# Macaron block (FFN, quaternion memory, FFN): the memory's output bias moved from a TensorE product into the centred output weights

## The reference, cut to what matters

```python
B, L, D = x.shape                      # 2, 4096, 256
keys = (x @ Wk.T + bk).reshape(B, L, N_QUAT, 4)
keys = keys / jnp.maximum(knorm, NORM_EPS)
values = (x @ Wv.T + bv).reshape(B, L, N_QUAT, 4)
bound = quat_mul(values, keys)
memory = jnp.cumsum(bound, axis=1)
retrieved = quat_mul(memory, quat_conj(keys)).reshape(B, L, D)
retrieved = retrieved / jnp.sqrt(positions)[None, :, None]
mu = jnp.mean(retrieved, axis=-1, keepdims=True)
var = jnp.var(retrieved, axis=-1, keepdims=True)
normed = (retrieved - mu) / jnp.sqrt(var + LN_EPS) * ln_g + ln_b
return x + (normed @ Wo.T + bo)
```

## Time and profile before

| | us |
|---|---|
| three runs, median (lowest to highest) | 648.37 (646.26 to 649.11) |
| the profiled execution, its own time | 648.11 |
| its span, first to last instruction | 646.4 |

### The profile page before, as it was taken

How to read it: one execution, slowest core, us unless ns; L and a number is a source line. 1 busy time by engine, 2 the same in 40 slices (tenths; PEclk the granted TensorE clock), 3 DMA queues, 4 the chain that set the end, 5 groups by cost and what they waited for, 6 DMA issues and landing times.

```text
span 646.4 us, 12285 instructions
## 1 busy us (share of the span) xinstructions
PE 612.6 (95%) x3341; PEld 521.1 (81%) x3341; DVE 565.1 (87%) x1168; ACT 468.2 (72%) x858; POOL 539.8 (84%) x626
## 2 busy tenths in 40 slices
PE   6989999999987999999999999998877999999997
PEld 5878989989865787777878787777666899898996
DVE  6979999998869999999999999999848788787773
ACT  5666776767567888888888888887365777677662
POOL 4588898897848999999999999998826988889863
PEclk9989999999999999999999999999899999999999
DMA  8740000000000000000000000000000110110111
GB/s 251 238 132 1 0 0 0 0 0 1 1 1 1 1 2 0 0 0 0 0 0 0 0 0 0 0 1 0 2 0 2 67 65 32 65 65 32 65 66 66
DMA packets 19273, 18.66 MB, mean 29 GB/s; under 512 B 1328, under 2 KB 19248, under 8 KB 19248
## 3 DMA queue, kind: packets, MB, share of 16 engines
q1 hardware_dynamic: 19248, 18.36, 8.8%
HBM read 9.97 MB, written 8.39 MB: 28 GB/s over the span
## 4 chain that ended last, share of the span: by engine, by line
PE 45%; POOL 25%; issue 18%; DVE 7%; ACT 3%; POOLq 1%; DMA 0%; DVEq 0%; ACTq 0%
PE bank L1228 25%; PE bank L1259 16%; POOL rhalf L286 7%; POOL ret L293 6%; POOL kact L275 5%; POOL bhalf L268 4%; PE bank L1242 4%; POOL bhalf L266 1%; ACT xn L778 1%; POOL rhalf L284 1%; DVE xk L410 1%; POOL xr_lo L1084 1%; DVE xn L613 1%; DVE kact L418 0%; POOL rstd L1077 0%
## 5 line engine op out<-in xcount | busy, mean ns | idle before, releaser
L1259 PE MATMUL bank<-wffn,kact 128*128 128x256 f32 x512 | 118.0, 384 | 6.5 <-DVE kact L418 4.1
L1318 PE MATMUL bank<-wkv,m_xnT 128*128 128x256 f32 x480 | 116.4, 385 | 2.4 <-ACT m_xnT L882 2.4
L1259 PEld LDWEIGHTS bank<-wffn,kact 128*128 128x128 f32 x512 | 96.0, 192 | 19.5 <-DVE kact L418 4.5
L1318 PEld LDWEIGHTS bank<-wkv,m_xnT 128*128 128x128 f32 x480 | 88.8, 190 | 24.2 <-ACT m_xnT L882 8.8
L299 POOL TENSOR_TENSOR xk_lo<-xk,xk_hi 128x1024 fp32r<-128x1024 f32 x30 | 71.1, 2370 | 43.7 <-ACT xk_hi L786 43.4
L1091 POOL TENSOR_TENSOR res<-res,gating_buffers 128x1024 f32 (+1 forms) x31 | 74.6, 2408 | 13.5 <-DVE gating_buffers L425 13.0
L1084 POOL TENSOR_TENSOR xr_lo<-xr,xr_hi 128x1024 fp32r<-128x1024 f32 x32 | 76.0, 2374 | 7.6 <-ACT xr_hi L792 6.2
L613 DVE TENSOR_TENSOR xn<-bank,khat 128x1024 f32<-128x1024 f32 x64 | 77.7, 1216 | 2.2
L778 ACT ACTIVATE xn<-res,shift,rstd 128x256 f32 (+1 forms) x128 | 66.5, 592 | 15.3 <-POOL shift L1079 11.0
L613 DVE TENSOR_TENSOR gating_buffers<-bank,khat 128x1024 f32<-128x1024 f32 x64 | 77.4, 1211 | 0.0
L1228 PE MATMUL bank<-wffn_hi,xr_hi 128*128 128x256 f32 x256 | 72.1, 282 | 0.0
(11 more groups left out here) (135 smaller groups left out, 1603.8 us busy)
## 6 DMA issues: line engine op xcount, KB each, us to landing
res<-x SPq DMA_DIRECT2D x15, 512.0 KB, 4.2
out<-res SPq DMA_DIRECT2D x15, 512.0 KB, 2.9
res<-x SPq DMA_DIRECT2D x2, 256.0 KB, 2.9
out<-res SPq DMA_DIRECT2D x2, 256.0 KB, 2.2
wffn<-w_k SPq DMA_DIRECT2D x1, 256.0 KB, 4.6
wffn<-w_r SPq DMA_DIRECT2D x1, 256.0 KB, 5.3
wo<-w_o SPq DMA_DIRECT2D x1, 256.0 KB, 5.6
wffn<-w_v SPq DMA_DIRECT2D x1, 256.0 KB, 5.8
```

What stands on the lines that cost most here:

```text
L1259: last = nc.tensor.matmul(dst[:, i, :], x[:, f, i * P:(i + 1) * P], wffn[:, w, f, :], start=f == 0, stop=f == FC - 1)
L1318: last = nc.tensor.matmul(dst[:, i, :], m_xnT[:, f, i * P:(i + 1) * P], wkv[:, f, col:col + D], start=False, stop=f == FC - 1, skip_group_ ...
```

## The change

The bias is added without a product of its own. The row of the bias, divided by 256, is added to each of the 256 rows of `wo_centred`. To the transposed `normed` one is added in each element. The product is then normed @ W + 1 @ W + normed @ bias/256 + 1 @ bias/256 = normed @ W + 0 + 0 + bias, since each column of W sums to zero, and each row of `normed` must now sum to zero too. For that `normed` is shifted as well as scaled, by `n_shift` = -mean x `n_rstd`, which DVE computes behind the reciprocal.

- PE: L1376 falls away (two products a step). One product of 128 x 256 is added behind L1401, which writes the bias as a row into every partition of PSUM.
- DVE: `ln_inverse` gets a wait on its own reciprocal and one `scalar_tensor_tensor` of 128 x 2 (inputs `n_mv` and `n_rstd`, both in SBUF); `rstd_done` is now signalled by that one. `other_layernorms` gets a wait on PE's new product and two `scalar_tensor_tensor` of 128 x 256, from PSUM and SBUF into `wo_centred`.
- ACT: `ret_normalize` gets a bias operand of one column; `evict_nT` turns from a copy into an Identity activation with a bias of one.
- POOL: one memset at setup.

```diff
@@ ln_inverse (DVE) @@
                 def ln_inverse(j, b):
                     dve.wait_ge(m["std_done"], 2 * j + b + 1)
-                    nc.vector.reciprocal(n_rstd[:, b, :], n_std[:, b, :]).then_inc(m["rstd_done"], 1)
+                    nc.vector.reciprocal(n_rstd[:, b, :], n_std[:, b, :]).then_inc(m["inverse_done"], 1)
+                    dve.wait_ge(m["inverse_done"], 2 * j + b + 1)
+                    nc.vector.scalar_tensor_tensor(n_shift[:, b, :], n_mv[:, b, :, 0], -1.0, n_rstd[:, b, :],
+                                                   ALU.mult, ALU.mult).then_inc(m["rstd_done"], 1)
@@ other_layernorms (DVE) @@
                 x_scales(1, CT, NT - CT)
                 memory_stats(NJ - 1, 1)
+                dve.wait_ge(out_bias_summed, 1)
+                for f in range(FC):
+                    nc.vector.scalar_tensor_tensor(wo_centred[:, f, :], bank[3][:, 0, 0:D], 1.0 / D, wo_centred[:, f, :],
+                                                   ALU.mult, ALU.add).then_inc(mem_ready, 1)
@@ ret_normalize, evict_nT (ACT) @@
-                        last = nc.scalar.activation(normed[:, i, :], ret[:, b, i, :], ACT.Identity, scale=n_rstd[:, b, i:i + 1])
+                        last = nc.scalar.activation(normed[:, i, :], ret[:, b, i, :], ACT.Identity, bias=n_shift[:, b, i:i + 1],
+                                                    scale=n_rstd[:, b, i:i + 1])
-                    nc.scalar.copy(normedT[:, :, :], rt_bank).then_inc(m["normedT_done"], 1)
+
+                    nc.scalar.activation(normedT[:, :, :], rt_bank, ACT.Identity, bias=one[:, 0:1]).then_inc(m["normedT_done"], 1)
@@ prepare (POOL) @@
+                nc.gpsimd.memset(one[:, :], 1.0)
@@ output (PE) @@
+                    pe.wait_ge(mem_ready, 2 * FC)
                     need(pe, m["x_done"], s)
                     for i in range(2):
                         for f in range(FC):
-                            nc.tensor.matmul(o_bank[:, i, :], normedT[:, f, i * P:(i + 1) * P], wo_centred[:, f, :],
-                                             start=f == 0, stop=False)
-                        last = nc.tensor.matmul(o_bank[:, i, :], ones[:, :], bias3[:, 2 * D:], start=False, stop=True)
+                            last = nc.tensor.matmul(o_bank[:, i, :], normedT[:, f, i * P:(i + 1) * P], wo_centred[:, f, :],
+                                                    start=f == 0, stop=f == FC - 1)
                     last.then_inc(m["O_done"], 1)
@@ first_values (PE) @@
                     nc.tensor.matmul(bank[3][:, 1, :], ones[:, :], bias3[:, 0:2 * D], start=True, stop=True).then_inc(kv_bias_summed, 1)
+                    nc.tensor.matmul(bank[3][:, 0, 0:D], ones[:, :], bias3[:, 2 * D:], start=True, stop=True).then_inc(out_bias_summed, 1)
```

More of the change, by code:

```diff
@@ L164, in macaron @@
         n_rstd = sb("n_rstd", [P, 2, 2])
+        n_shift = sb("n_shift", [P, 2, 2])
+        one = sb("one", [P, 1])
         m_xn = sb("m_xn", [P, 2, D])
@@ L217, in macaron @@
         kv_bias_kept = sem("kv_bias_kept")
+        out_bias_summed = sem("out_bias_summed")
         lnb_folded = sem("lnb_folded")
@@ L233, in macaron @@
         ffn_sems = [{n: sem(f"f{i}_{n}") for n in FFN_SEMS} for i in range(2)]
-        MEM_SEMS = ["x_st_done", "x_mv_done", "x_moments_done", "x_var_done", "x_power_done", "x_std_done", "x_rstd_done", "x_scales_done", "st_done", "mv_done", "std_done", "rstd_done", "xn_done", "T_done", "xnT_done",
+        MEM_SEMS = ["x_st_done", "x_mv_done", "x_moments_done", "x_var_done", "x_power_done", "x_std_done", "x_rstd_done", "x_scales_done", "st_done", "mv_done", "std_done", "inverse_done", "rstd_done", "xn_done", "T_done", "xnT_done",
                     "res_done", "K_bias_done", "V_bias_done", "K_done", "V_done", "ksq_done", "ksum_done", "above_done", "knorm_done",
```

## The result

The kernel after takes 664.02 us, the median of four executions (662.82 to 664.55), where the kernel before took 648.74 beside it (646.26 to 649.18). The ratio is 1.0241, with a 95% interval of 1.0211 to 1.0271. The forecast was 664.4.

What follows compares the result with a forecast made beforehand. DVE was taken to bound the memory stage. From 648.1 us, 14.5 for the shift, 1.6 for the bias row, 0.3 for ACT and -0.2 for PE gave 664.3, stated as 664.4, range 656.5 to 667.5.

Steps and rivals of the forecast that it cites:

- What bounds the stage: Memory stage: DVE bounds it, so added DVE work is paid in full 32 times and PE's saving is worth nothing.
- ACT's longer forms: Bias operands in ret_normalize and evict_nT: 0.3 us a step, hidden by ACT's idle time; 0.3 us in the last step.
- The -0.2 for the product in the peeled steps: Bias product ahead of the last but one store_x, where DVE waits for PE: removing it saves 0.2 us.
- The hold: Shift instruction in ln_inverse, held to POOL's next start: 0.49 us in each of 26 steps, 12.8; chance 0.75.
- steps 1 and 2: First two memory steps, POOL in another phase: 0.33 us for both, bounds 0 and 1.0.
- steps 28, 30 and 32: Late memory steps with POOL about to run dry or idle: 0.2, 0.24 and 0.25 us for the shift.
- The Trainium skill's rule that I weighed: VectorE with two SBUF inputs contends with GpSimd reading SBUF; the second is blocked for the other's whole instruction.
- step 31: Last but one memory step: POOL's instruction begins ahead of the new one, so the shift costs 0.69 us, unheld 0.22.
- The bias row: Between first FFN and memory: PE's new product and two DVE instructions delay key_sum 1.6 us, bounds 0.8 and 2.0.
- The mark that I gave for it: Sign for the bias row at the memory's start: key_sum starts near 193.3, where it was 191.67.
- The rival without the hold: Shift instruction of 128x2 not held, costing its own 0.22 to 0.25 us a step: 657.2 us; chance 0.13.
- Four fp32 products are 0.86: PE's output, 0.97 us a tile: four fp32 products take 0.86, so the bias product takes 0.11.

Runs made afterwards that it cites:

- b_stat128: Kernel before plus one bn_stats over 128 columns of wkv on DVE ahead of the reciprocal; 657.54 us, ratio 1.0129.
- b_no_product: Kernel before without its 64 bias products of output, the output bias left out; 646.04 us, ratio 0.9989.
- a_no_shift: Kernel after without the shift's wait and instruction on DVE, a column of zeros as ACT's bias; 651.87 us, ratio 1.0068 against the kernel before.
- a_psum_input: Kernel after with the new instruction's first input read from PSUM instead of n_mv in the memory's steps; 661.04 us, ratio 1.0208 against the kernel before.
- a_stat128: Kernel after plus one bn_stats over 128 columns of wkv on DVE ahead of the reciprocal; 668.26 us, ratio 1.0306 against the kernel before.
- a_stat384: Kernel after plus one bn_stats over 384 columns of wkv on DVE ahead of the reciprocal; 686.2 us, ratio 1.0591 against the kernel before.
- a_warm: Kernel after with idle products in PE's two gaps, 12 behind the bias row, 5 and 9 near the end; 665.63 us, ratio 1.028 against the kernel before.
- a_shift_on_act: Kernel after with the shift computed on ACT, DVE keeping the reciprocal alone; 653.32 us, ratio 1.0077 against the kernel before.
- a_pad4: Kernel after plus four one-column memsets on DVE ahead of the reciprocal; 667.8 us, ratio 1.0325 against the kernel before.

## Why the prediction was right, point by point

**What bounds the stage: right, and shown.** DVE bounds the memory steps. 0.20 us put on it cost 0.20 a step (b_stat128), and PE's products taken away gained nothing there (b_no_product). ACT's longer forms cost nothing in the steps: recip 1 to 27 is unchanged in a_no_shift, where they are in. They measured 587 ns for `normed` and 691 for `normedT` (493 and 588 before), as the same form had foretold. At the end of the stage they were to cost 0.3 us, and behind the last reciprocal a_no_shift has 0.29 over before. The -0.2 for the product in the peeled steps is there as well: b_no_product's last step is 9.64 us for 9.86.

**The hold: right, and shown.** The steps were to be 9.03 us and are 9.02, the new instruction 0.4 to 0.5 us and is 0.42, POOL's wait 0.7 and is 0.73. From the first to the 27th reciprocal I had 12.1 us more and there are 12.09. That match is closer than its parts: steps 1 and 2 cost 0.64 us where I had 0.33, and the 24 behind them 11.45 (0.48 each) where I had 11.76. a_psum_input separates the instruction's own 0.22 from the hold's 0.26; a_stat128 and a_stat384 show that it goes by POOL's boundaries. Over all 32 steps the hold applied where POOL was at work, and in steps 28, 30 and 32, with POOL idle, the instruction took 0.16 us. The Trainium skill's rule that I weighed, "SBUF — State Buffer", section "Who interferes with whom", held: with two inputs in SBUF the small instruction was blocked (0.42 us), with one it was not (0.16). In step 31 the forecast was 0.69, and it is there on DVE:

```profile
481.35 0.72 POOL L296 TENSOR_TENSOR ret<-rhalf 128x256 f32<-128x256 f32 x1
...
481.47 0.62 DVE L588 SCALAR_TENSOR_TENSOR n_shift<-n_mv,n_rstd 128x2 f32<-128x2 f32 x1
482.01 0.73 DVE L413 SCALAR_TENSOR_TENSOR xk<-diff,cols_less_one,bank 128x512 f32<-128x512 f32 x1
```

**The bias row: right in size.** DVE's wait and the two instructions, and PE's product ahead of them (timeline):

```profile
189.74 0.27 PE L1415 MATMUL bank<-bias,ones 128*128 128x256 bf16 x1
...
190.05 0.75 DVE L739 SCALAR_TENSOR_TENSOR wo_centred<-bank,wo_centred 128x256 f32<-128x256 f32 x2 [0.82 <-PE bank L1415]
190.73 0.68 DVE L600 TENSOR_REDUCE ksum<-ksq 128x128 f32<-128x512 f32 x1
```

From the first x_mv to key_sum it is 0.29 us in the kernels with the old start and 1.85 to 1.88 in all those with the new one. That is 1.58 in the kernel after, where I had 1.6. The mark that I gave for it, key_sum near 193.3, was missed all the same: it starts at 190.73, since the stage ahead of it ended 2.5 us earlier.

**What lies ahead of the memory: missed.** I took the stage ahead as fixed. It was 2.5 us shorter (x_mv at 188.86 for 191.38), and not by the change: b_no_product, whose edits lie in the memory alone, has the same. The traces show two causes, and neither comes from the change. One is the held `eps_pos`. The other is the clock: behind PE's idle time at 34 to 38 us of the span it was 0.50 between 38 and 40 us in four of the fourteen profiled executions, and 1.00 in the other ten. The products at that place in a_psum_input and in a_warm (timelines of PE):

```profile
36.09 5.41 PE L1275 MATMUL bank<-wffn,kact 128*128 128x256 f32 x16 [1.89 <-DVE kact L421]
```

```profile
37.74 3.72 PE L1272 MATMUL bank<-wffn,kact 128*128 128x256 f32 x16 [2.03 <-DVE kact L421]
```

Between POOL's second and third update of `res` there are 11.10 to 11.12 us in the four executions with the lower clock and 9.86 to 9.87 in the ten without. From that third update to x_mv it is 135.8 to 136.0 us in all fourteen. The four combinations all occur. With both causes (before, b_stat128, a_shift_on_act) x_mv starts at 191.4 to 191.5; with the hold alone (a_warm) and with the clock alone (a_psum_input) at 190.0; with neither, in nine kernels, at 188.0 to 188.9. So each is worth 1 to 2 us, and kernels whose code up to there is nearly the same differ in which of them they have. What makes the one or the other happen in an execution isn't settled. The length of PE's idle time ahead of the products isn't what decides, since the clock fell behind 1.89 us and not behind 2.03.

**PE's clock at the two ends: missed.** The forecast had nothing for it. From key_sum to the first reciprocal it is 0.5 us in the kernel after, and in the table 0.5 to 1.5 in every kernel with the bias row against 0.0 to 0.2 in those without. In all of the former but a_warm PE is idle for 3.29 us ahead of its transposes, and the clock falls to 0.50 behind it; how long it stays there differs. a_warm kept the clock, but its 0.7 us come from idle products that ended late, so no run gives the price of the idle time at the start by itself. For the five intervals from the 27th to the 32nd reciprocal the forecast's terms were 0.49, 0.20, 0.49, 0.24 and 0.69 - 0.2 = 0.49; they came out 0.48, 0.22, 0.47, 0.20 and 1.99. Only the last is off, by 1.5, and the slow key products make 1.55 of it (4.45 - 2.90). In a_pad4, where the clock stayed up, the last term came out 0.45 (10.31 - 9.86). The Trainium skill, "TensorE: Matmul & The Clock Gate", section "Loop structure matters more than you think", warns that long waits between products let PE go cold. The windows agree: 0.50 behind the idle time. I had asked what the change does to PE's work and not what it does to its idle time. With the idle time filled the clock stayed up (a_warm); but the idle time doesn't bring the fall in each execution, as a_pad4 shows. The last step is anywhere from 10.3 to 12.9 us in the kernels that have the shift on DVE, and the kernel before with a pad (b_stat128) has 12.63.

**The sum was right partly by luck.** By the same cuts the forecast was 1.6 up to key_sum, 0, 12.1, 1.9 and 0.55 behind the last reciprocal, 16.2 in all; measured were -0.94, 0.47, 12.09, 3.36 and 0.52, 15.5 in all. The terms of the change itself are right within 0.1, steps 1 and 2 aside (0.3, made up by the steady steps). Beside them a gain of 2.5 us ahead of the stage and losses of 0.5 and 1.5 to the clock at its ends, none of them foreseen, nearly cancelled. The rival without the hold, at 657.2, has fallen by the steps; a_psum_input, where there is no hold but in step 31, came to 661.04, which is 3.8 us more: its price too left out the clock.

**A slip in the text.** "Four fp32 products are 0.86" counts four loads, which belong to two products of 0.43 us each. The bias product's 0.11 came from the difference and is not touched. b_no_product's PE is busy 4.6 us less in some 25 steps, 0.18 a step where two of them make 0.22.

## What to carry to other kernels

Before a small instruction is put on an engine, look at where its inputs lie and what POOL is doing at that point. A DVE instruction of two elements a partition with both inputs in SBUF cost 0.48 us a step, wait included, where POOL never rests; the same with one input in PSUM cost 0.22, and on an engine with idle time, ACT, 0.02. And when work moves away from PE, or a wait is put ahead of it, price the clock that its idle time can cost and not only the work saved.

## What the runs showed of the hardware

- The held instruction lets go at the boundary between two POOL instructions that follow each other without a gap: DVE's next starts within 0.02 us of POOL's next (352.90 and 352.90; 354.53 and 354.54). So its cost depends on phase: in the steady step a pad of 0.20 us cost nothing and one of 0.47 cost 0.69.
- The hold goes the other way too. POOL's cast of 128x6, which takes 0.19 us else, took 1.27 in the kernel after, at 16.63, where a DVE instruction with two SBUF inputs started in the same hundredth and lasted 1.22.
- Memsets of one column on DVE cost about 0.01 us each in a row, while a reciprocal of 128x2 costs 0.07, and one waited for by the next instruction 0.19 to 0.20.
- A product of 128x256 in fp32 is two instructions and 0.43 us of PE at full clock, twice what its columns suggested to me.
- The granted clock fell to 0.50 behind PE's idle times of 1.36 and 2.22 us with 0.66 us of work between them, and not behind one of 2.28 alone in the kernel before; products then started every 0.43 instead of 0.23 us. The idle times don't settle it: it stayed up behind 1.01 and 2.22 us (a_pad4) and fell behind 0.58 and 2.22 (a_stat128), and in the first FFN it stayed up behind 2.03 us (a_warm) and fell behind 1.89 (a_psum_input).
